# Twelve pairs in split precision, layer 2's split terms a slot behind, and another spread of GpSimd's work

## What is computed

```python
e = stack([tbl_f[ids[:, f]] for f in range(39)], axis=1)        # 2048 x 39 x 16
x0 = xk = e
for idx, (W, b) in enumerate([(w0, b0), (w1, b1), (w2, b2)]):
    z = relu(einsum('bhd,bkd,hks->bsd', x0, xk, W) + b[None, :, None])   # 128 maps
    if idx != 2:
        xk = z[:, :64, :]; direct.append(z[:, 64:, :])
    else:
        direct.append(z)
logit = sum(concatenate(direct, axis=1), axis=-1)               # 2048 x 256
h = maximum(concatenate([logit, dense_ctx], axis=1) @ W_top1 + b_top1, 0)
h = maximum(h @ W_top2 + b_top2, 0)
y = h @ W_top3
```

## Time and profile before

| | us |
|---|---|
| median of 3 runs | 2543.55 (2541.47 to 2548.54) |
| the profiled execution, its own time | 2545.02 |
| its span in the profile | 2543.1 |
| TensorE busy | 2432.8 |
| VectorE busy | 2268.7 |
| GpSimd busy | 1557.9 |
| ScalarE busy | 1175.5 |

### The profile page before, as it was taken

One profiled execution on the slowest core, in us unless ns is written; L12 is line 12 of the kernel. 1 busy time (PEld: TensorE's weight loads), 2 busy tenths in 40 slices (PEclk: granted clock), 3 DMA queues, 4 the chain that ended last, 5 costly groups with the idle time before them and its releaser, 6 DMA issues.

```text
span 2543.1 us, 25999 instructions
## 1 busy us (share of the span) xinstructions
PE 2432.8 (96%) x7712; PEld 1423.5 (56%) x7712; DVE 2268.7 (89%) x1356; ACT 1175.5 (46%) x1414; POOL 1557.9 (61%) x1029
## 2 busy tenths in 40 slices
PE   0599999999999999999999999999999999999999
PEld 0265555556555555555555565555556555555553
DVE  0599999999999999999999999999999999999960
ACT  0244444445454444545444444444444444445442
POOL 6476667667666766766676666667666766743240
PEclk9899999999999999999999999999999999999999
DMA  2986777777677777867777776787777677766610
GB/s 69 246 211 180 199 207 202 180 217 214 176 198 205 207 178 215 209 182 197 209 206 177 217 206 190 190 211 210 178 207 205 200 184 213 207 182 194 195 30 0
DMA packets 262712, 477.02 MB, mean 188 GB/s; under 512 B 19500, under 2 KB 37788, under 8 KB 262614
## 3 DMA queue, kind: packets, MB, share of 16 engines
q1 hardware_dynamic: 141766, 271.07, 38.9%
q10 hardware_dynamic: 100480, 200.29, 28.5%
q0 software_dynamic: 20448, 5.45, 1.4%
HBM read 468.99 MB, written 7.74 MB: 187 GB/s over the span
## 4 chain that ended last, share of the span: by engine, by line
PE 73%; POOL 10%; DVE 6%; issue 4%; DMA 4%; ACT 2%; SPq 0%; POOLq 0%; DVEq 0%; ACTq 0%
PE z L693 37%; PE z L716 33%; POOL emb L352 5%; DVE prod L418 4%; POOL pair_lo L211 4%; DMA emb<-in_tbl,idx 3%; PE xk L775 1%; PE z L775 1%; DMA x_pairs<-x_transposed 1%; ACT pair_hi L532 1%; POOL half_parts L207 1%; DVE pair_lo L211 1%; PE turned L674 1%; DVE logit L448 1%; ACT xk L542 0%
## 5 line engine op out<-in xcount | busy, mean ns | idle before, releaser
L418 DVE TENSOR_TENSOR prod<-x_pairs,xk 128x2048 f32<-128x2048 f32 x640 | 1436.4, 2284 | 75.2 <-PE z L716 46.9
L693 PE MATMUL z<-prod,w_plain 128*128 128x512 f32 (+2 forms) x2944 | 1383.1, 594 | 40.5 <-DVE prod L418 40.5
L532 ACT CAST pair_hi<-prod 128x1024 fp32r<-128x1024 f32 x703 | 735.4, 1046 | 1085.2 <-PE z L716 793.6
L211 POOL TENSOR_TENSOR pair_lo<-prod,pair_hi 128x1024 fp32r<-128x1024 f32 x320 | 764.1, 2388 | 638.3 <-ACT pair_hi L532 621.7
L693 PEld LDWEIGHTS z<-prod,w_plain 128*128 128x128 f32 (+2 forms) x2944 | 555.4, 189 | 474.1 <-issue 394.9
L352 POOL DMA_INDIRECT emb<-in_tbl,idx x624 | 701.3, 1124 | 184.0 <-issue 173.7
L716 PE MATMUL z<-pair_hi,w_lo 128*128 128x512 f32 (+1 forms) x1408 | 786.6, 559 | 2.3 <-DVE pair_lo L211 1.7
L716 PE MATMUL z<-pair_hi,w_hi 128*128 128x512 f32 (+1 forms) x1408 | 555.7, 395 | 0.0
L716 PE MATMUL z<-pair_lo,w_hi 128*128 128x512 f32 (+1 forms) x1408 | 555.1, 394 | 0.0
L211 DVE TENSOR_TENSOR pair_lo<-prod,pair_hi 128x1024 fp32r<-128x1024 f32 (+1 forms) x384 | 468.5, 1220 | 48.7 <-ACT pair_hi L532 48.7
L716 PEld LDWEIGHTS z<-pair_hi,w_lo 128*128 128x128 f32 (+1 forms) x1408 | 265.2, 188 | 297.2 <-POOL pair_lo L211 135.8
(11 more groups left out here) (50 smaller groups left out, 566.5 us busy)
## 6 DMA issues: line engine op xcount, KB each, us to landing
x_pairs<-x_transposed SPq DMA_DIRECT2D x64, 2432.0 KB, 16.9
x_pairs<-x_transposed ACTq DMA_DIRECT2D x64, 2432.0 KB, 19.3
x_diag<-x_transposed SPq DMA_DIRECT2D x128, 546.0 KB
x_diag<-x_transposed ACTq DMA_DIRECT2D x64, 546.0 KB
x_pairs<-x_transposed SPq DMA_DIRECT2D x64, 256.0 KB, 20.4
emb<-in_tbl,idx POOLq DMA_INDIRECT x624, 6.3
x_diag<-x_transposed SPq DMA_DIRECT2D x128, 78.0 KB
x_transposed<-stage SPq DMA_DIRECT2D x32, 156.0 KB
```

Of the source, the lines that this page charges most:

```text
L211: engine.tensor_tensor(pair_lo[0:rows, pair % PAIR_RING], held[0:rows, at:at + 2, :], pair_hi[0:rows, pair % PAIR_RING].bitcast(F32), ALU. ...
L418: nc.vector.tensor_tensor(prod[0:rows, pos % RING, 0:n, :], a, xk.unsqueeze(1).broadcast_to([rows, n, N]), ALU.mult).then_inc(prod_ready, 1)
L532: nc.scalar.copy(pair_hi[0:rows, pair % PAIR_RING], held[:, at:at + 2, :]).then_inc(hi_ready, 1)
L693: ins = nc.tensor.matmul(z[n][:], w, held[0:rows, i, :], start=(k == 0 and i == plain[0]), stop=(k == last_slot and not here and i == plai ...
```

## The change

- **Layer 0 gets a second split pair** (slot 0, tiles 2 and 3), so a chunk has 12 pairs. On TensorE a new `layer0` waits for both slots of layer 0 at once, takes the second slot's three plain tiles, then the four split tiles of the first, and frees both slots together at its end.
- **Layer 2's split terms come a slot behind** (`BEHIND`): TensorE takes slot k's plain tiles, then slot k-1's split tiles, and frees slot k-1 then.
- **The low part of layer 1's pair in slot 1 goes to GpSimd.** VectorE keeps four pairs and the half tile of layer 1 and has two pairs of layer 0: seven low parts in a chunk, as before.
- **The parts' rings hold six tiles** (`hi_parts`, `lo_parts`), three pairs in place of two.
- **ScalarE writes the high parts of layer 1's that VectorE subtracts a second time, to PSUM** (`hi_copy`, `direct01[0:HALF]`), and VectorE reads the high part there. `hi_copy` takes the banks of the transposes (`turned`). ScalarE waits for VectorE's earlier low part before it overwrites `hi_copy`. VectorE's low part of slot 0 comes before the third product (it came after it).
- **`direct01` is in PSUM** (it was in SBUF). xk0 shares a bank with xk2, so ScalarE waits for layer 0's second product before it writes xk2.
- **The logit rows in SBUF are cut to a window** of a group; SyncE stores each window to HBM once a group and `load_top` loads them again (10 DMAs in place of 6).
- **Gathers**: 24 ahead, then 12, 3, 12, 12 over the four chunks, each lot between GpSimd's layer-1 low part and its layer-2 low parts. The next indices are loaded at the end of chunk 1.
- **The transposes come behind layer 0**, and ScalarE's `fill_stage` comes behind `direct_0` inside layer 2's splits.

The core of the diff:

```diff
-SPLITS = {0: [(0, 0, 2)],
-          1: [(0, 0, 2), (1, 0, 2), (2, 0, 2), (2, 3, 1), (3, 0, 2), (4, 0, 2)],
-          2: [(0, 0, 2), (1, 0, 2), (2, 0, 2), (2, 3, 1), (3, 0, 2), (4, 0, 2)]}
-EARLY = {1: 4, 2: 4}
+SPLITS = {0: [(0, 0, 2, V), (0, 2, 2, V)],
+          1: [(0, 0, 2, V), (1, 0, 2, G), (2, 0, 2, V), (2, 3, 1, V), (3, 0, 2, V), (4, 0, 2, V)],
+          2: [(0, 0, 2, G), (1, 0, 2, G), (2, 0, 2, G), (2, 3, 1, G), (3, 0, 2, G), (4, 0, 2, G)]}
+EARLY = {1: 5, 2: 4}
+BEHIND = {1: False, 2: True}
-GATHERS_AHEAD = 30
-GATHERS_AT = [range(30, F), range(0, 10), range(10, 20), range(20, 30)]
-PAIR_RING = 2
+GATHERS_AHEAD = 24
+GATHERS_AT = [range(24, 36), range(36, F), range(0, 12), range(12, 24)]
+PARTS = 6
...
-        direct01 = sb("direct01", [P, N])
-        logit01 = sb("logit01", [P, B])
-        logit2 = sb("logit2", [P, CB + B])
+        logit01 = sb("logit01", [P, NB])
+        logit2 = sb("logit2", [P, NB])
...
+        hi_copy = ctx.enter_context(nc.psum_tensor("hi_copy", [P, 2, N], F32))
+        turned = [hi_copy[:, 0, :], hi_copy[:, 1, :]]
+        direct01 = ps("direct01")
         xk1, xk2 = ps("xk1"), ps("xk2")
+        xk0 = xk2
...
+                hi = (hi_copy[0:rows, 0:m, :] if copy else
+                      hi_parts[0:rows, place:place + m, :].bitcast(F32))
+                engine.tensor_tensor(lo_parts[0:rows, place:place + m, :], held[0:rows, at:at + m, :],
+                                     hi, ALU.subtract).then_inc(done, 1)
...
+                    if c == 0:
+                        sp.wait_ge(summed01, bt * CHUNKS + 1)
+                        store_window(0, bt)
+                    if c == 1:
+                        sp.wait_ge(summed2, bt * CHUNKS + 2)
+                        store_window(1, bt)
                     if c == 2 and not last:
                         store_group(bt + 1)
...
+                    done = lows_of(1, chunk, 0, split, pos)
+                    if c == 2 and len(fields_at[c]):
+                        start_group(bt + 2, False)
+                    gather(fields_at[c])
...
+                    lows_of(2, chunk, done, split, pos)
...
+                    if n and who == V:
+                        copies = [s for s in SPLITS[n][0:i] if s[3] == V]
...
+                            nc.scalar.copy(hi_copy[:, 0:m, :].bitcast(F32R), held[:, at:at + m, :]
+                                           ).then_inc(hi_copied, 1)
...
-                        act.wait_ge(summed01, chunk + 1)
+                        act.wait_ge(summed01, chunk + 2)
                         direct_0()
-                        pair = round_splits(SPLITS[2][EARLY[2]:], P, slot, pos, pair, held_by)
+                        if c == 1 and not last:
+                            fill_stage(bt + 1)
...
+                    if not BEHIND[n]:
+                        split_parts(n, k, lows)
+                    elif k > 0:
+                        split_parts(n, k - 1, lows)
+                if BEHIND[n]:
+                    split_parts(n, last_slot, lows)
```

364 lines of the change are left out of this document (212 added, 152 removed).

## The result

The changed kernel took 2747.8 us (median of 4 runs, 2740.2 to 2749.4) where the kernel before took 2546.0: a ratio of 1.079 (95% interval 1.076 to 1.082). I had forecast 2481. The profiled run took 2740.2 us with a span of 2738.5.

A forecast was written before the change was run, and what follows sets the result against it. TensorE bounds the kernel, with VectorE close behind. 48 periods lose 1.00 us and 15 lose 1.35, taken as 67; late bands add 4: 2545 - 67 + 4 = 2482, at the median 2481; range 2470 to 2523.

The forecast's parts named there:

- TensorE's need: TensorE's work in a chunk if it never waits: 35.67 us after the change, 36.60 with the transposes.
- VectorE: VectorE's need in a chunk: 35.02 us, 0.65 below TensorE's; `sum01` at 0.69, nothing charged for low parts reading PSUM.
- The walk through layer 2: Layer 2 a slot behind: low parts come 0.5 to 1.6 us early, so TensorE's 0.67 us of standing goes.
- the layer-1 low part on GpSimd: GpSimd's layer-1 low part runs from 20.4 to 22.8 us after layer 1's end; TensorE wants it at 25.3.
- the freed slots: Layer 2's slots freed later: VectorE wants slot 2 at 15.6 and gets it at 16.3; its slack pays the 0.7.
- the double casts: ScalarE's second casts in layer 1: VectorE waits 0 to 0.1 us, and today's 0.77 goes.
- the transposes: Transposes behind layer 0, in chunk 1: 1.02 us of TensorE standing go, 0.93 us of work stay.
- Gathers: Twelve GpSimd gathers, 1.25 us each, end about 3 us into the next chunk, before layer 2's first low part at 5.0.
- one stretch: One lengthened gather allowed per twelve, beside VectorE low parts with both operands in SBUF; today some take 1.60 and 1.78.
- Stage later: Later `fill_stage` moves store and bands; bands issue at 18.3, not 8.4; cost 0 to 2.3 us a group, taken 0.3.
- rival 2: Bands land late in chunk 1: 1 to 2.3 us in each of 15 groups, 2492 to 2512 us; 17%.
- alone: Band loads with no other load beside them: done 8.3 us later, at 26.6 after layer 1's end.

The follow-up runs named there:

- e16: Changed kernel with the next group's store behind bands and pair loads, gathers 10, 9, 10, 10, and three unused semaphores allocated first: 2485.1 us, ratio 0.977.
- job D: Third follow-up job, on a chip of its own, where e9 and e11 ran; the kernel before took 2549.7 us there.
- e11: e5 with GpSimd's gathers of a chunk waiting for layer 1's third product: 2526.7 us, ratio 0.992.
- e9: e1 with three unused semaphores allocated ahead of the others: 2508.8 us, ratio 0.985.
- e14: e1 run again unaltered in another job: 2500.8 us, ratio 0.983.
- e13: Changed kernel run again unaltered in another job: 2628.7 us, ratio 1.033.
- e4: Changed kernel without its loop's gathers (output not the reference's): 2629.2 us, ratio 1.032.
- C, D and E: Follow-up jobs, each on its own chip; the kernel before took 2549.2, 2549.7 and 2545.2 us there.
- e1: Changed kernel with the next group's store issued behind the bands and pair loads: 2592.7 us, ratio 1.018.
- e18: Changed kernel, store still ahead of the bands, with the pair loads of c=2 held until the bands have landed: 2625.7 us, ratio 1.032.
- e2: Changed kernel with gathers 10, 9, 10, 10 over the four chunks: 2695.4 us, ratio 1.058.
- e3: Changed kernel with the edits of both e1 and e2: 2529.8 us, ratio 0.993.
- e17: e3 run again unaltered in another job: 2527.4 us, ratio 0.994.
- A, B and F: Jobs: the first measurement (chip not on record) and two follow-up jobs; the kernel before took 2546.0, 2546.7 and 2544.1 us there.
- job B: First follow-up job, where e1, e2, e3 and e4 ran; the kernel before took 2546.7 us there.
- e5: e1 with layer 1's slot-1 low part on VectorE again: 2525.8 us, ratio 0.991.
- e12: e5 with the gathers of e2 (10, 9, 10, 10): 2515.8 us, ratio 0.987.

## Why the prediction was wrong, step by step

- **TensorE's need, right.** 35.67 and 36.60 us were worked out; where nothing disturbs it TensorE runs at 35.80 and 36.67. With 0.1 us a chunk this leaves the 2485.1 of e16 against the forecast 2481. (e16 is the changed kernel with two edits; the agreement is of TensorE's pace, not of the kernel that was forecast.)
- **VectorE, right.** Low parts from PSUM at 1.21 us, `sum01` 0.68. The rule on PSUM's access time, in the Trainium skill's Perfetto Trace Analysis, Optimizing Scalar/DVE Operations, would by its 60 and 125 ns make each such low part some 0.06 us dearer, an estimate; no row here shows that, 1.210 beside 1.215 with both operands in SBUF.
- **The walk through layer 2, the layer-1 low part on GpSimd, the freed slots, the double casts, the transposes: right.** e16 has no wait of TensorE in four chunks, and over the whole run VectorE waits 2.8 us for copies in PSUM. What GpSimd's low part is worth is seen in job D, e11 beside e9: 18 us.
- **Gathers, half right.** They take 0.94 us beside the low parts that read PSUM, as forecast. The "one stretch" was mis-sized: two low parts of layer 0 stand in a row now, and the gather beside them takes 2.5 to 3.7 us. The walk's margin takes that up in c=0 and c=3, but the burst of c=2 starts behind the index load, which I had left out: 1.3 us a group. From e14 to e16, 15.7 us.
- **Stage later, the step that failed.** The mechanism stood there as rival 2, and the bands' issue was placed within 0.1 us. The landing was mis-sized: up to 33 after layer 1's end, where it was 37.4. I counted one 2.4 MB load beside the bands, ScalarE's, and forgot SyncE's own, which stands right behind the bands. In the kernel before that one went out at 1060.58, as the bands issued at 1052.90 were ending (1061.2 in the forecast's reading), because it waited for a product; with the bands 10 us later its product is long there, and it goes out at once:

```profile
1060.58 0.68 SPq L226 DMA_DIRECT2D x_pairs<-x_transposed  x1
```

  So the 8.3 us that I took for "alone" were alone only thanks to that wait. By my own measure of 9 us for a half, a second half adds up to 9: a landing at up to 42 and a stand of up to 11 us, where 37.4 and some 8 came. That was to be had from the rows. (The forecast's own terms are uneven: ScalarE's half first gives 25.5 + 8.3 = 33.8, not 33, and 33 less 31.0 is 2.0, not 2.3.) The clock then added 1.5 and 0.8 us, which I had not priced. The term that I put at 0.3 us a group is 8.5: 128 us.
- **Late counts, not foreseen.** No term of the forecast stands for them. 2747.8 - 2628.7 = 119 us, between two jobs with the same program. Either of these last two would alone have taken the time past 2523.

The parts add up, 4 + 16 + 128 + 119 = 267 = 2748 - 2481, but they must: they are the steps from the forecast to e16, e14, e13 and the changed kernel. In another order they split otherwise. While the bands are late, the burst of twelve costs nothing (chunk 2 of e13 is no longer than that of e4), so the late bands alone are worth 2628.7 - 2485.1 = 144 us, 9.6 a group.

What stays open is why TensorE's counts come late. It can be read from every trace: xk2's ReLU starts 0.20 us behind TensorE's first record of layer 0 wherever counts are on time. In chunks 2 and 3 that is so, or less, in the kernel before, in e4 and in every run of C, D and E. The changed kernel, e1 and e18 have 3.3 to 3.9 us there on average, with twelve gathers; e2, e3 and e17 have 1.4 to 1.6, with ten. So it differs between jobs for one and the same program (A, B and F late, C, D and E not), it needs the gathers (e4, in job B), and there it grows with their number. In chunk 1 it does not: 0.4 us with twelve (e1), 0.2 with ten (e3); that burst starts some 5 us later, behind the index load.

The late jobs have a second mark. The trace of each changed kernel there holds 3628 to 5226 of the 9984 landings of gathers, in C, D and E 9963 or more. e4 in job B lacks half of its 1248 as well, without a late count. So recording itself suffers in those jobs; whether it has a part in the late counts is not shown, as every time here is of a recorded execution. Since jobs B to F had a chip each, chip and occasion are not told apart. Whether GpSimd's layer-1 low part is needed for it is open too, as e5, e11 and e12 fell into jobs without it. The kernel before took 2544 to 2550 us in every job, so the lateness is nothing that its times show; its trace was read in one job only.

## What to carry to other kernels

When a load is moved, price everything that stands behind it on its queue by the wait that holds it back, and ask whether that wait still holds at the new time: "alone" in the old trace may be the work of a wait that the move makes void. Here a load was due in 13 us, in a chunk with 36.7 us of work, and had no room for 5 MB beside it.

When an edit that changes no work moves the time by 3%, run the unaltered kernel again before explaining anything. "Remote" as the releaser, in a kernel on one core, and missing landing times of the pair loads on the page were the sign here that a run's counts were late (those of the gathers are missing on the changed kernel's page in every job); two kernels should be compared only where both have it or neither.

When parts are priced by taking fixes away one after another, look whether one stall hides another before calling a difference the price of one cause.
